# VectorE's output sum placed ahead of marking and weighing, and another order of the opening, in a convolution and routed low-rank kernel

## What is computed

```python
# conditional convolution: 4 groups of 8 channels, 9 taps, along L = 512
y = conv1d(x, weight, groups=4, padding=4) + (cond @ c_weight.T)[:, :, None] + bias[None, :, None]
# feed-forward with routes: rows of 512 elements
base   = y @ base_W.T + base_b                      # 512 x 512
probs  = softmax(y @ router_W.T + router_b)         # 15 routes
p, i   = top_k(probs, 8)
w      = sum of p over the chosen routes of each of 8 experts   # expert_map
h      = y @ A.T                                    # 8 experts x rank 16
out    = x + base + 2.0 * ((h * w) @ B)             # 128 -> 512
```

## Time and profile before

| | |
|---|---|
| median of three runs | 201.86 us |
| the profiled execution | 201.71 us |
| its span, first to last instruction | 199.6 us |
| TensorE matmul (PE) busy | 184.2 us, 92%, 1246 matmuls |
| VectorE (DVE) busy | 160.7 us, 81% |
| POOL busy | 145.3 us, 73% |
| ScalarE (ACT) busy | 76.8 us, 38% |
| DMA | 31.89 MB, mean 160 GB/s |
| granted TensorE clock, mean | 1.00 of full |
| chain of waits, share of the span | PE 44%, DVE 36%, POOL 7%, issue 6%, DMA 2% |

### The profile page before, as it was taken

One profiled execution on the slowest core, in us unless ns is written; L12 is line 12 of the kernel. 1 busy time (PEld: TensorE's weight loads), 2 busy tenths in 40 slices (PEclk: granted clock), 3 DMA queues, 4 the chain that ended last, 5 costly groups with the idle time before them and its releaser, 6 DMA issues.

```text
span 199.6 us, 4275 instructions
## 1 busy us (share of the span) xinstructions
PE 184.2 (92%) x1246; PEld 173.5 (87%) x1246; DVE 160.7 (81%) x551; ACT 76.8 (38%) x214; POOL 145.3 (73%) x135
## 2 busy tenths in 40 slices
PE   7879978999999899998999899998999999999993
PEld 2457967989989898998989899998989899899992
DVE  0499989788888879878887979888897988888673
ACT  4654444442333444433244444233344443322210
POOL 2529999977789777777988777778877787774520
PEclk9999999999999999999999999999999999999999
DMA  6989234656545363646536465654435432333313
GB/s 201 308 317 381 61 113 156 216 156 210 157 142 186 100 167 147 210 158 176 157 124 176 113 203 158 192 175 139 156 106 186 151 105 105 108 105 105 107 56 105
DMA packets 17867, 31.89 MB, mean 160 GB/s; under 512 B 2112, under 2 KB 3008, under 8 KB 17856
## 3 DMA queue, kind: packets, MB, share of 16 engines
q1 hardware_dynamic: 17136, 31.28, 49.4%
q10 hardware_dynamic: 720, 0.49, 0.8%
HBM read 23.36 MB, written 8.39 MB: 159 GB/s over the span
## 4 chain that ended last, share of the span: by engine, by line
PE 44%; DVE 36%; POOL 7%; issue 6%; DMA 2%; DVEq 1%; ACT 1%; ACTq 0%
PE wide_ps L593 29%; DVE xr L723 6%; PE wide_ps L627 5%; DVE y L812 5%; PE conv_banks L579 5%; DVE terms L759 3%; DVE y_rows L752 3%; DVE y_rows L749 3%; DVE y_rows L745 3%; DMA cond_in_sb<-cond 2%; PE hwt_bank L579 2%; DVE spread L789 2%; DVE expert_w L793 2%; POOL x_lo L223 2%; DVE hw_lo L824 2%
## 5 line engine op out<-in xcount | busy, mean ns | idle before, releaser
L593 PE MATMUL wide_ps<-wide_hi,y_hi 128*128 128x400 f32 (+1 forms) x248 | 80.4, 329 | 8.0 <-DVE xr L723 6.7
L593 PE MATMUL wide_ps<-wide_lo,y_hi 128*128 128x400 f32 (+1 forms) x248 | 76.3, 312 | 0.1
L593 PE MATMUL wide_ps<-wide_hi,y_lo 128*128 128x400 f32 (+1 forms) x248 | 76.3, 312 | 0.0
L482 POOL TENSOR_TENSOR terms_lo<-terms,terms_hi 128x512 fp32r<-128x512 f32 x28 | 36.2, 1294 | 29.2 <-ACT terms_hi L374 29.1
L593 PEld LDWEIGHTS wide_ps<-wide_hi,y_hi 128*128 128x128 f32 x248 | 46.3, 188 | 12.4 <-issue 8.5
L593 PEld LDWEIGHTS wide_ps<-wide_lo,y_hi 128*128 128x128 f32 x248 | 46.5, 189 | 0.4 <-DVE wide_lo L835 0.3
L593 PEld LDWEIGHTS wide_ps<-wide_hi,y_lo 128*128 128x128 f32 x248 | 46.3, 188 | 0.0
L477 POOL TENSOR_TENSOR xr<-xr,biases_sb 128x512 f32<-128x512 f32 x32 | 41.4, 1293 | 6.1 <-DMA xr<-x_rows 6.1
L500 POOL TENSOR_TENSOR y_lo<-y,y_hi 128x512 fp32r<-128x512 f32 x31 | 40.1, 1295 | 2.0 <-ACT y_hi L389 2.0
L396 ACT ACTIVATE hw_hi<-hwt_bank 128x128 fp32r<-128x128 f32 x31 | 8.6, 278 | 82.7 <-PE hwt_bank L614 82.7
L389 ACT ACTIVATE y_hi<-y 128x512 fp32r<-128x512 f32 x32 | 20.2, 632 | 17.7 <-PE wide_ps L593 13.1
(11 more groups left out here) (92 smaller groups left out, 316.9 us busy)
## 6 DMA issues: line engine op xcount, KB each, us to landing
xr<-x_rows SPq DMA_DIRECT2D x32, 256.0 KB, 3.6
out<-xr SPq DMA_DIRECT2D x31, 256.0 KB, 3.0
terms<-x_units SPq DMA_DIRECT2D x28, 256.0 KB, 2.7
edges<-x_edges SPq DMA_DIRECT2D x14, 256.0 KB, 3.0
wide_sb<-wide_w SPq DMA_DIRECT2D x4, 328.0 KB, 5.3
x_in<-x_first SPq DMA_DIRECT2D x4, 264.0 KB, 4.3
conv_sb<-conv_w SPq DMA_DIRECT2D x2, 192.0 KB, 5.9
biases_sb<-biases SPq DMA_DIRECT2D x1, 263.5 KB, 5.9
```

The costliest lines, as they stand in the source:

```text
L482: nc.gpsimd.tensor_tensor(terms_lo[i % 2][:, :, :, :], terms[i][:, :, :, :], terms_hi[i % 2][:, :, :, :].bitcast(F32), ALU.subtract)\
L593: mm = nc.tensor.matmul(sums_of(t, k)[:, b, 0:columns[1] - columns[0]], a[k % 2][:, r, :], w[:, r, columns[0]:columns[1]], start=r == 0 an ...
```

## The change

On VectorE, a step of the loop is now: condition and turn of t+2, logits of t, hw_low of t-1, the eight best of t, difference of t+4, **add_out of t-1**, mark and weigh of t. The negated maximum is no longer a reduction on VectorE but a copy with scale -1 of the first of the eight best on ScalarE. The reciprocal is behind the weight. `hw_low` no longer waits for `top_ready`. TensorE's steps from 2 on are unchanged.

In the opening, `cond` is issued second on ScalarE's queue and has the router bias in it; `base_b` is a transfer of its own behind `up`; the condition's bias is added by ScalarE with Identity; the expert map is copied and compared on VectorE behind tile 1's turn; y_low of tile 1 goes to VectorE; tile 1's front sums come ahead of the conv of tile 3 (`second_step`); one warm-up matmul less; VectorE's and POOL's first two steps are in another order; the turns of tiles 2 and 3 wait for `y_hi_ready`, as their buffers' low parts were made on VectorE itself.

```diff
-WARM_UP, WARM_BETWEEN = 9, 3
+WARM_UP, WARM_BETWEEN = 9, 2
...
             load_terms(START, 0)
-            sync.dma_start(biases_sb[:, :], biases.partition_broadcast(P)).then_inc(biases_in, 16)
...
             sync.dma_start(up_sb[:, :], up_w).then_inc(up_in, 16)
+            sync.dma_start(base_b_sb[:, :], base_b.partition_broadcast(P)).then_inc(base_b_in, 16)
...
         def _(act):
...
+            load_conv(0)
+            act.dma_start(cond_in_sb[:, :], cond).then_inc(cond_in, 16)
+            load_conv(1)
             act.wait_ge(zeros_ready, 1)
             nc.scalar.activation(zero_exp[:, :], zeros[:, 0:1], ACT.Exp)
-            act.dma_start(cond_in_sb[:, :], cond).then_inc(cond_in, 16)
...
+            def bias_condition(n):
+                act.wait_ge(cond_summed, n + 1)
+                for g in range(2 * n, 2 * n + 2):
+                    nc.scalar.activation(cond_sb[:, g, :], cond_ps[:, g, :], ACT.Identity,
+                                         bias=conv_b_sb[:, g:g + 1]).then_inc(cond_biased, 1)
+
             def exponentials(t, k):
+                act.wait_ge(top_ready, t + 1)
+                nc.scalar.activation(minus_best[k % 2][:, :], top[k % 2][:, 0:1], ACT.Copy,
+                                     scale=-1.0).then_inc(best_ready, 1)
                 act.wait_ge(best_ready, t + 1)
...
             x_high(1)
-            wide_high(range(1, RUNS - 1))
+            bias_condition(0)
+            wide_high(range(1, 2))
             y_high(0, 0)
-            wide_high(range(RUNS - 1, RUNS))
+            wide_high(range(2, RUNS))
             conv_high(2)
             x_high(2)
             x_high(3)
+            bias_condition(1)
...
             def step(t, k, p, q):
+                if isinstance(t, int) and t == 1:
+                    hw_high(0, 0)
                 if from_tile(t, 1) and up_to_tile(t, TILES - 2):
                     y_high(t + 1, k + 1)
...
-            y_low(1, 1, 2)
             edge(START // 2, 0)
             conv_low_later(3)
...
                     terms_low(t + 4, k)
                     edge_low(p + 2, k // 2)
-                    pool.wait_ge(biases_in, 16)
+
+                    y_low(t + 2, k + 2, 3)
+                    pool.wait_ge(base_b_in, 16)
                     bias_rows(t, k)
                     return
                 if isinstance(t, int) and t == 1:
+                    bias_rows(t, k)
+                    edge(p + 3, 1 - k // 2)
+                    terms_low(t + 4, k)
+                    y_low(t + 2, k + 2)
+                    conv_low_later(4)
+                    return
...
             def conv_first_late(t):
+                pe.wait_ge(y_rows_ready, t - 1)
+                pe.wait_ge(conv_hi_ready, 3)
+                pe.wait_ge(x_hi_ready, t + 1)
+                conv_first(t, (X_HIGH,))
+                pe.wait_ge(conv_lo_ready, 2)
+                conv_first(t, (X_W_REST,))
                 pe.wait_ge(x_lo_ready, t)
-                pe.wait_ge(conv_lo_ready, 2)
-                pe.wait_ge(y_rows_ready, t - 1)
-                conv_first(t).then_inc(conv_done, 1)
+                conv_first(t, (X_REST,)).then_inc(conv_done, 1)
...
                 conv_first_late(2)
+
+            def second_step():
+                runs = range(RUNS)
+                pe.wait_ge(y_hi_ready, 2)
+                linear(1, 1, runs, (FRONT_BANK,), (HIGH,))
+                linear(1, 1, runs, (FRONT_BANK,), (W_REST,))
+                pe.wait_ge(y_lo_first, 2)
+                linear(1, 1, runs, (FRONT_BANK,), (Y_REST,)).then_inc(front_done, 1)
                 conv_first_late(3)
+                turn_hw(0, 0)
+                linear(1, 1, runs[:3], (NEXT_BANK,))
+                up(0, 0)
+                linear(1, 1, runs[3:], (NEXT_BANK,)).then_inc(linear_done, 1)
...
-                dve.wait_ge(logits_ready, t + 1)
-                nc.vector.tensor_reduce(minus_best[i][:, :], logits[i][:, :], AX_X, ALU.max,
-                                        negate=True).then_inc(best_ready, 1)
+
+            def best(t, k):
+                i = k % 2
                 nc.vector.max(top[i][:, :], logits[i][:, :]).then_inc(top_ready, 1)
...
                 dve.wait_ge(exps_ready, t + 1)
-                nc.vector.reciprocal(inv[i][:, :], total[i][:, :]).then_inc(inv_ready, 1)
                 dve.wait_ge(rest_ready, t + 1)
...
+                nc.vector.reciprocal(inv[i][:, :], total[i][:, :]).then_inc(inv_ready, 1)
...
             def hw_low(t, k):
-
-                if from_tile(t, 1) and up_to_tile(t, TILES - 2):
-                    dve.wait_ge(top_ready, t + 2)
                 dve.wait_ge(hw_hi_ready, t + 1)
...
             wide_low(0)
+            dve.wait_ge(cond_biased, 2)
+            condition_first(0)
+            turn(0, 0)
+            wide_low(1)
+            y_low(0, 0)
+            wide_low(2)
+            wide_low(3)
+            condition_first(1)
+            turn(1, 1)
+            dve.wait_ge(map_in, 16)
+            nc.vector.tensor_copy(map_f[:, :], map_i[:, :]).then_inc(map_ready, 1)
...
+            choose(0, 0)
+            dve.wait_ge(logits_ready, 1)
+            best(0, 0)
             difference(START, 0)
...
+            y_low(1, 1)
             dve.wait_ge(is_expert_ready, E)
             weigh(0, 0)
+            dve.wait_ge(cond_biased, GROUPS)
...
                 if isinstance(t, int) and t == 0:
+                    condition_first(2)
+                    turn(2, 2)
+                    choose(1, 1)
+                    dve.wait_ge(logits_ready, 2)
+                    best(1, 1)
...
+                    dve.wait_ge(top_ready, 2)
+                    mark(1, 1)
+                    hw_low(0, 0)
+                    weigh(1, 1)
+                    return
                 if isinstance(t, int) and t == 1:
                     add_out(0, 0)
+                    condition_first(3)
+                    turn(3, 3)
+                    difference(START + 1, 1)
+                    return
...
+                if up_to_tile(t, TILES - 2):
+                    choose(t, k)
+                    dve.wait_ge(logits_ready, t + 1)
+                    hw_low(t - 1, k - 1)
+                    best(t, k)
+                    if up_to_tile(t, TILES - 5):
+                        difference(t + 4, k)
                     dve.wait_ge(top_ready, t + 1)
-                if up_to_tile(t, TILES - 1):
+                    if up_to_tile(t, TILES - 3):
+                        add_out(t - 1, (k - 1) % UNROLL)
                     mark(t, k)
                     weigh(t, k)
-                if from_tile(t, 2) and up_to_tile(t, TILES - 3):
-                    add_out(t - 1, (k - 1) % UNROLL)
```

More of the change, by code:

```diff
@@ L51, with build @@
 W_PIECES = (slice(0, 2), slice(2, 4), slice(4, 8), slice(8, 11), slice(11, 14))
-def build(nc, x_first, x_units, x_edges, x_rows, conv_w, cond, wide_w, up_w, biases, expert_map, out):
+def build(nc, x_first, x_units, x_edges, x_rows, conv_w, cond, wide_w, up_w, base_b, expert_map, out):
     ctx = ExitStack()
@@ L516, in step @@
                 if isinstance(t, int) and t == 1:
-                    y_low(t + 1, k + 1)
-                    bias_rows(t, k)
-                else:
-                    if up_to_tile(t, TILES - 1):
-                        bias_rows(t, k)
-                    if up_to_tile(t, TILES - 2):
-                        y_low(t + 1, k + 1)
+                    bias_rows(t, k)
[4 more added lines that the diff above has]
+                    return
+                if up_to_tile(t, TILES - 1):
+                    bias_rows(t, k)
+                if from_tile(t, 3) and up_to_tile(t, TILES - 2):
+                    y_low(t + 1, k + 1)
                 if up_to_tile(t, TILES - 5):
@@ L702, in step @@
                     first_step()
+                elif isinstance(t, int) and t == 1:
+                    second_step()
                 else:
@@ L809, in turn @@
                 dve.wait_ge(y_rows_ready, t + 1)
-                if from_tile(t, 2):
+                if isinstance(t, int) and t < 4:
+                    if t >= 2:
+                        dve.wait_ge(y_hi_ready, t - 1)
+                else:
                     dve.wait_ge(y_lo_ready, t - 1)
@@ L885, in step @@
                                                    op1=ALU.subtract).then_inc(up_lo_ready, 1)
-                    return hw_low(0, 0)
+                    dve.wait_ge(top_ready, 2)
[3 more added lines that the diff above has]
+                    return
                 if isinstance(t, int) and t == 1:
                     add_out(0, 0)
-                if up_to_tile(t, TILES - 5):
-                    difference(t + 4, k)
-                if up_to_tile(t, TILES - 1):
+                    condition_first(3)
[3 more added lines that the diff above has]
+                if up_to_tile(t, TILES - 3):
+                    condition(t + 2, (k + 2) % GROUPS, q + (k + 2) // GROUPS)
+                    turn(t + 2, k + 2)
```

(6 more changed lines are left out.)

69 lines of the change are left out of this document (21 added, 48 removed).

## The result

The changed kernel takes 206.38 us, median of four runs (205.38 to 208.35), against 201.86 before (201.64 to 201.94): the ratio is 1.024, with a 95% interval of 1.015 to 1.032. It is slower, where I forecast 200.6 with a range to 203.0; whether by more than 2% the interval leaves open. The four runs differ in TensorE's granted clock, and that is needed to read them: 205.38 and 205.58 at 0.997, 207.19 at 0.990, 208.35 at 0.983. The profiled execution is the one of 205.58.

A forecast was written before the change was run, and what follows sets the result against it. Neither TensorE nor VectorE alone was taken as the bound; after the change, a ring between them at 5.69 us a tile. Opening 34.1 + steady 148.5 + ending 15.8 = 198.4, plus 2.1 and 0.15: 200.6 us, range 198.0 to 203.0.

The forecast's parts named there:

- The steady part: The 26 steps from turn(2) to turn(28): 26 x 5.71 = 148.5 us, against 147.91 before.
- The wait for the emptied bank: TensorE's 12 waits, 6.0 us, for the output sum that empties its PSUM bank pair: claimed to go.
- the ring of condition, turn, up and output sum: Steady part, VectorE and TensorE waiting on each other: 1.39 + 2.10 + 0.11 + 2.09 = 5.69 us a tile.
- The reciprocal, behind the weight instead of ahead of it, was inside a wait for the marking anyway: VectorE, steady part: moving the reciprocal was claimed to change nothing in the ring.
- The term that I did carry for the loop: VectorE's L745, address from a register: 0 to 0.07 us in 20 tiles, up to +1.4; +0.02 a tile taken.
- The opening: Everything up to turn(2): a gain of 1.8 us, bounds 0.7 and 2.4.
- the map copy and the comparisons ... cost it up to 0.9 there, which lies in the same wait: VectorE in the opening, ahead of tile 0's choice: up to 0.9 us, hidden inside a wait.
- that contention: Opening: POOL and VectorE excluding each other, y_low(1) up to 1.3 us longer; up to 1.0 put into the late values.
- turn(2): TensorE's transpose of tile 2's weighed rows, the opening's end: forecast at 34.1 us, 35.87 before.
- the falling clock: Rival: clock falls in TensorE's 2.5 us hole in the opening, costing 1.5 us, 202.1; 4%.
- The ring longer than its sum: Rival, steady part: 5.80 a tile from two waits in a row ahead of L799, L723 and L745; 203.0 us, 20%.
- The ending: From turn(28) to the end of the span: order kept, 15.8 us as before.

The follow-up runs named there:

- e1: The changed kernel with the reciprocal put back ahead of the weight; 204.99 us, ratio 1.017 to the kernel before.
- e2: The changed kernel with the wait for the exponentials moved ahead of the output sum, reciprocal still behind the weight; 205.36 us, ratio 1.020 to the kernel before.
- e10: The changed kernel with reciprocal ahead of the weight, no loop, map copy and comparisons early, six matmuls on zeros in TensorE's hole; 200.09 us, ratio 0.993.
- e3: The changed kernel with its loop written out; 205.32 us, ratio 1.019 to the kernel before.
- e4: The kernel before with its loop written out; 199.50 us, ratio 0.989.
- e6: The changed kernel with the map copied by POOL and the eight comparisons earlier on VectorE; 204.91 us, ratio 1.015 to the kernel before.
- e8: The changed kernel's opening with the steady part of before; ten runs, 201.02 and 201.36 us, eight of 202.36 to 202.85, ratio 1.003 to the kernel before.
- e5: The kernel before with the changed steady part alone, opening of before; 206.74 us, ratio 1.024.
- e7: The changed kernel with twelve matmuls on zeros in TensorE's hole ahead of conv(4); 205.49 us, ratio 1.019 to the kernel before.
- e9: The new opening with steady part of before, map copy and comparisons early, six matmuls on zeros in TensorE's hole; 199.75 us, ratio 0.990 to the kernel before.
- e11: The new opening with steady part of before, map copy and comparisons early, six matmuls in the hole, no loop; 198.01 us, ratio 0.982 to the kernel before.

## Why the prediction was wrong

**The steady part: the mechanism was right, two terms were missing.** The wait for the emptied bank went, and the ring of condition, turn, up and output sum took its place, with both waits where the prediction put them. Its 5.69 a tile is what e1, e2 and e10 measure. Two steps failed.

- "The reciprocal, behind the weight instead of ahead of it, was inside a wait for the marking anyway." It was, but moving it put two waits ahead of one instruction, and the second one costs 0.07 to 0.08 a step. Without the loop's edges in the way, e3 against e10 gives 149.96 - 148.17 = 1.8 us for the 26 steps. I had named two waits in a row ahead of L799, L723 and L745 as a reason for the longer ring, and not this pair, the one pair that the change makes new. e1 and e2 show the cause.
- The edge of the loop was in no term. I took 26 equal steps. The condition is now on the ring and is the first instruction behind the edge, so each edge counts in full: 6.41 + 6.15 + 6.14 + 6.14 - 4 x 5.77 = 1.8 us (0.26 of it is the gap ahead of the reciprocal), and e3 takes out 1.93. The row to read was in the profile before: the steps between turns there are 5.53, 5.81, 5.48, 6.06, so a pair at the edge is 0.2 longer than its neighbour. I had measured one average over it, 5.69, and that average hid what a loop costs.

1.79 and 1.93, with 0.26 by which e10's steady part is still longer than that of before (its ring measures 5.70, the steps of before 5.69), are the whole 3.98 by which the steady part grew. The term that I did carry for the loop, 0 to 0.07 for an address from a register, came out at its lower end: the changed kernel's ordinary steps inside the loop, 5.76 to 5.80, are those of e3, which has no loop. That the ring's sum equals a step of before was chance, and it hid what the order costs: of the steps of before, 1.85 in 147.91 was the loop's (e4), so the order of before, without the loop, is 2.1 us shorter than the ring.

**The opening: right in its first third, then given back.** VectorE's first condition came at 8.35 (forecast 8.1 to 8.4) and TensorE's first long sum at 10.68 (10.5 to 10.8). The step that failed is "the map copy and the comparisons ... cost it up to 0.9 there, which lies in the same wait". I took their durations from where they stood before, where POOL had pauses, and moved them beside POOL's longest stretch; they took 3.5 us. I did weigh that contention, and applied it to y_low(1) alone, which then took 0.68, since it had been pushed into a pause of POOL. From there the delay ran on through the chain that the timelines show: choice of tile 0, ScalarE's exponentials, its conv_hi behind them, POOL's conv_lo at 19.53, and everything on POOL behind that, to the row of x that the output sum of tile 0 waited for (1.25) until 25.43. The prediction had POOL done at 23.3 to 24.0, and in e6, with the nine instructions moved, the output sum starts at 23.99. In the changed kernel turn(2) came at 35.86. With the nine instructions moved and the hole filled (and the reciprocal back and the loop written out) it comes at 33.94 (e10), against my 34.1.

**The hole and the clock.** The forecast had TensorE idle for about 2.5 us ahead of conv(4); it was 3.09. I gave the falling clock 4% and 1.5 us. For one fall the size was right: e8's two groups are some 1.5 apart. The runs at 0.981 to 0.983 of the changed kernel, e2 and e3 lie 2.7 to 3.1 above those at 0.997 to 1.000, twice as much; where their clock fell no profile shows. The chance was not right: it fell in 23 of 31 runs of the kernels with this hole, and in 2 of the changed kernel's 4. My ground, that no hole of before is as long, was an absence of evidence, read as evidence for "mostly stays".

**The ring longer than its sum**, given 20% and 203.0, was the rival that came nearest, with steps of 5.77, just over its own point of decision (5.76), but for another pair of waits than the three it named; the loss went beyond it since edges, opening and clock all had the same sign, and I had let each stand alone. ScalarE's Identity needed no other table, as the Trainium skill says ("ScalarE: Activation LUTs", section "Table sets: the hidden batching unit"): the changed kernel has one table load, 1.28 us long, as in the earlier trace rows. The ending was right to 0.25. Without the clock, the four misses are 3.4 + 1.8 + 0.25 - 0.3 = 5.1 us, from 200.45, the forecast for a profiled execution (200.6 less the 0.15 to the median), to 205.58.

## What to carry to other kernels

When an edit makes a new chain the one that sets the pace, cost not only its instructions but what sits between them: how many waits each instruction has ahead of it, and whether the loop's edge now lies on it. Read single steps at and away from the edge, never one average over them.

An instruction that is moved doesn't keep its duration: look up what the other engines do where it lands, for each short instruction singly. And an idle stretch of TensorE of 3 us can have a price behind it, here 1.5 us in most runs, even where it costs nothing itself; here six matmuls on zeros took it away.

## What the runs showed of the hardware

- *A second wait ahead of a VectorE instruction* cost 0.07 us here (0.27 against 0.20 from marking to weight), although what it waits for was done 1.0 us earlier (ScalarE's exponentials end at 67.56 in the round shown above, the weight starts at 68.56). Moved to where VectorE waits anyway, it cost nothing (e2).
- *The end of a loop's body* cost VectorE 0.35 to 0.38 us each time, from the last instruction's start to the next one's, in the changed kernel, e2, e5 and e7 alike, and 0.21 to 0.24 in e1. A whole step at an edge was longer by 0.38 here, by 0.64 the first time; in e1 by 0.23 to 0.28 (and once by 0.3 behind the loop), in e2 by 0.36 to 0.40, in e5 by 0.49 and 0.75 the first time. The rest beyond the edge lies in gaps ahead of the reciprocal or the weight in the same step; why they come is open.
- *Short instructions with one SBUF input were held beside POOL as well.* The cast took 1.20 on VectorE and 0.20 on POOL in e6; the first of the comparisons took 1.25, and all eight 2.33 against 0.70 in e6, where POOL has nothing to do beside them. In VectorE's timeline, 13 to 16 us:

```profile
15.22 1.25 DVE L890 TENSOR_SCALAR is_expert<-map_f 128x15 f32<-128x15 f32 x1
```

The cast ends at 15.19, where the first of POOL's two x_lo ends (13.84 + half of 2.61), and the first comparison at 16.47, the end of the second. The Trainium skill, "SBUF — State Buffer", section "SBUF: two separate sides", has the exclusion not only for VectorE instructions with two inputs, but also for those in a mode that uses both ports. By that rule, the trace agrees, each of the two was held until POOL's current instruction had ended; in which mode they ran no row says.
- *The clock* went from 2.4 to 1.2 GHz behind 3.0 to 3.1 us without work on TensorE in three of six profiled executions with such a hole (granted clock from 27 to 30 us: 0.65 in e8, 0.56 in e1, 0.50 in e6) and stayed at 2.4 in the other three (the changed kernel, e2, e3). In e1 it fell as work began again, in e8 and e6 1.1 and 1.4 us after that. Of the unprofiled runs only the mean clock is known. In none of the twelve runs of e9, e10 and e11, with six matmuls and then a hole of 1.71 to 1.76 in that place (by their profiled executions), did it fall.
